# Attention with queries and keys projected transposed, stacked by DMA in two pieces, and two heads in the row halves of the array

## The reference

```python
qkv = (x @ Wqkv).reshape(b, l, 3, H, DH)          # b 8, l 512, H 16, DH 16
q, k, v = (qkv[:, :, 0], qkv[:, :, 1], qkv[:, :, 2])
q = q * cos + rotate_half(q) * sin                # rotate_half: (-second half, first half)
k = k * cos + rotate_half(k) * sin
scores = jnp.einsum('bqhd,bkhd->bhqk', q, k) * DH ** -0.5
attn = softmax(scores, axis=-1)
out = jnp.einsum('bhqk,bkhd->bqhd', attn, v).reshape(b, l, d)
x = layernorm(x + out @ Wo)
```

## Time and profile before

| | |
|---|---|
| runs of the kernel before | 1507.37 us median of 3 (1506.63 to 1508.64) |
| profiled execution | 1512.29 us, span 1510.5 us |
| TensorE busy | 1317.0 us, 87% |
| VectorE busy | 1044.7 us, 69% |
| ScalarE busy | 979.6 us, 65% |
| GpSimd busy | 518.4 us, 34% |
| granted TensorE clock, mean | 0.929 |

### The profile page before, as it was taken

The page is one execution under the profiler, slowest core; times in us unless marked ns, Lnnn a source line. Parts: engine busy times, 40 slices in busy tenths (PEclk is TensorE's granted clock), DMA queues, the critical chain, the costliest instruction groups (busy, mean ns, idle before and its releaser), DMA issues. The chain is left out here.

```text
span 1510.5 us, 30476 instructions
## 1 busy us (share of the span) xinstructions
PE 1317.0 (87%) x9849; PEld 1007.7 (67%) x9920; DVE 1044.7 (69%) x2129; ACT 979.6 (65%) x2014; POOL 518.4 (34%) x493
## 2 busy tenths in 40 slices
PE   3899999999999999689802989999999999997585
PEld 2544444444444443378702989999999999997485
DVE  3788877887888878387401557777777777775377
ACT  5588878887888888477301437666666666664265
POOL 6222212121222200064574004444444444445542
PEclk7799999999999999998955998999999999998698
DMA  8000010001000003320321006677777667762333
GB/s 335 1 1 29 2 31 1 30 1 31 2 29 2 15 1 112 123 74 18 109 104 70 0 19 233 221 221 237 238 231 239 220 219 236 235 217 63 101 102 95
DMA packets 113899, 160.46 MB, mean 106 GB/s; under 512 B 12928, under 2 KB 95872, under 8 KB 112640
## 3 DMA queue, kind: packets, MB, share of 16 engines
q1 hardware_dynamic: 107648, 142.32, 28.5%
q0 software_dynamic: 6144, 16.79, 3.5%
HBM read 121.86 MB, written 37.22 MB: 105 GB/s over the span
## 5 line engine op out<-in xcount | busy, mean ns | idle before, releaser
L470 DVE TENSOR_REDUCE att_mx<-att_psA 128x1 f32<-128x512 f32 x512 | 338.9, 682 | 62.0 <-PE att_psA L269 59.7
L387 ACT ACTIVATE att_prob<-att_psB 128x512 f32<-128x512 f32 x512 | 290.0, 602 | 81.4 <-PE att_psB L279 69.9
L1465 ACT ACTIVATE exp_psU<-exp_psU,ew_b 128x256 f32<-128x256 f32 x312 | 126.8, 444 | 154.2 <-PE exp_psU L1422 154.2
L269 PE MATMUL att_psA<-att_qk 96*128 96x512 bf16 x512 | 197.8, 388 | 8.9 <-DVE att_mx L470 5.3
L1497 DVE CAST exp_hh<-exp_psU 128x512 fp32r<-128x512 f32 x156 | 107.4, 688 | 110.2 <-ACT exp_psU L1465 110.2
L1420 PE MATMUL exp_psU<-exp_xh,exp_w1h 128*128 128x256 f32 x624 | 177.9, 285 | 2.1 <-DVE exp_w1l L1492 2.1
L1405 PE MATMUL exp_psD<-exp_w2h,exp_hh 128*128 128x256 f32 x624 | 179.6, 288 | 0.0
L1422 PE MATMUL exp_psU<-exp_xh,exp_w1l 128*128 128x256 f32 x624 | 177.5, 285 | 0.0
L1421 PE MATMUL exp_psU<-exp_xl,exp_w1h 128*128 128x256 f32 x624 | 177.5, 284 | 0.0
L279 PE MATMUL att_psB<-att_qk 128*128 128x512 bf16 x441 | 170.2, 387 | 7.8 <-issue 5.3
L1407 PE MATMUL exp_psD<-exp_w2h,exp_hl 128*128 128x256 f32 x624 | 176.5, 283 | 0.0
(11 more groups left out here) (186 smaller groups left out, 3344.1 us busy)
## 6 DMA issues: line engine op xcount, KB each, us to landing
ew_w<-ew SPq DMA_DIRECT2D x40, 1024.0 KB
exp_w<-ew SPq DMA_DIRECT2D x38, 1024.0 KB, 6.3
exp_xs<-slots_x SPq DMA_DIRECT2D x39, 256.0 KB, 6.1
slots_y<-exp_ys SPq DMA_DIRECT2D x39, 256.0 KB, 6.9
slots_x<-pre_acc SPq DMA_DIRECT2D x9, 1024.0 KB, 14.2
ew_b<-eb SPq DMA_DIRECT2D x39, 128.0 KB, 5.9
att_xt<-xT SPq DMA_DIRECT2D x8, 512.0 KB, 4.6
attn_rows<-att_ob SPq DMA_DIRECT2D x8, 512.0 KB, 3.2
```

Of the source, the lines that this page charges most:

```text
L269: pe.matmul(psA[A_BANK[n % U]][:, :], r[:, 0, qt * P:(qt + 1) * P], r[:, 1, :], start=True, stop=True).then_inc(s_amm, 1)
L387: act.activation(prob[:, n % PR, :], psB[n % 2][:, :], ACT.Exp, scale=SCALE).then_inc(s_exp, 1)
L470: dve.reduce_max(mx[:, g % 2, n % U:n % U + 1], psA[A_BANK[n % U]][:, :], AX_X).then_inc(s_max, 1)
```

## The change

Queries and keys are projected with the weights as the stationary operand, so that features lie in partitions and rows of the sequence in columns: no head has to be transposed. The weights' columns are reordered on the host, eight heads to a block, the even heads in the first 64 partitions and the odd ones in the last 64. A second product with rotated columns gives the rotated half. There are 32 blocks (four for each sequence: queries and keys of eight heads, twice), one to a period, each with twelve fp32r products of 512 columns in three steps. ScalarE copies both results out of PSUM, GpSimd multiplies with the tables, adds, and splits the sum into two fp32r pieces. SyncE writes the two pieces to memory (`bounce_block`) and reads them back with six DMAs into `qs` and `ks` (`stack_block`): three copies of 16 rows for each half, so that one fp32r product over 48 rows sums three products of pieces. Two more rows of `qs` take the two pieces of the negative maxima; these are transposed once, copied, written to memory and read back with two DMAs (`place_max`).

Both kinds of scores are now fp32r products over 48 or 50 rows, at partitions 0 to 63 for one head of a pair and 64 to 127 for the other. Row scores run A_LEAD = 29 steps ahead, and the order of the two kinds alternates, so that neighbouring matmuls are in different halves. There are two banks `psX`. The zeroing of the slots moves to the last seven periods of SyncE's queue, and the attention's outputs are loaded back after it. Ahead of the weight split VectorE sets the rows 32 to 63 of both halves of `ks` to one.

```diff
+    PAIRS = P // (2 * DH)
+    HALF = P // 2
+    KQ = 3 * DH
+    KM = KQ + 2
+    NB = 2 * D // P
+    BLOCKS = B * NB
+    SLOTS = 4
+    BOUNCE = 4
...
-    A_LEAD = U + 4
+    A_LEAD = U + 13
...
+    PROJECT_QK, EVICT_QK = (1, 2, 3), (3, 4)
+    SPLIT_MAX, TURN_MAX, COPY_MAX = 4, 6, 7
+    COPY_OUT, TURN_OUT, NORM_OUT = 5, 8, (10, 11)
+    PROJECT_V, COPY_V, SPLIT_X = 9, 11, 14
...
+    Q_PIECES, K_PIECES = (0, 1, 0), (0, 0, 1)
...
+        hl = a.sb("hl", [P, 2, 2, L], F32R)
+        qs = a.sb("qs", [P, SLOTS, PAIRS, L], F32R)
+        ks = a.sb("ks", [P, SLOTS, PAIRS, L], F32R)
...
+        mm = a.sb("mm", [P, P], F32)
+        mrow = a.sb("mrow", [2 * U, P], F32R)
...
-        psT = a.ps("psT", [P, 2, L], BF16)
-        psX = a.ps("psX", [P, 512], F32)
-        psXt = psX[:, :].bitcast(BF16)
+        psX = [a.ps(f"psX{i}", [P, L], F32) for i in range(2)]
...
+            def stack_block(i):
+                hb, kind = i // 2, i % 2
+                sp.wait_ge(s_out[kind], 16 * (hb + 1))
+                if hb == 0:
+                    sp.wait_ge(s_ones, 2)
+                if hb >= SLOTS:
+                    sp.wait_ge(s_bmm, 2 * U * (hb - SLOTS + 1))
+                if hb >= 1:
+                    sp.wait_ge(s_stk[kind], 96 * hb)
+                for half in range(2):
+                    src = qk_rows[i % BOUNCE, half * HALF:(half + 1) * HALF].rearrange("(j d) m l -> m d j l", d=DH)
+                    for m, piece in enumerate((Q_PIECES, K_PIECES)[kind]):
+                        dst = (qs, ks)[kind][half * HALF + m * DH:half * HALF + (m + 1) * DH, hb % SLOTS, :, :]
+                        sp.dma_start(dst.bitcast(F32), src[piece]).then_inc(s_stk[kind], 16)
+            def bounce_block(i):
+                sp.wait_ge(s_lo, i + 1)
+                if i >= BOUNCE:
+                    sp.wait_ge(s_stk[i % 2], 96 * ((i - BOUNCE) // 2 + 1))
+                sp.dma_start(qk_rows[i % BOUNCE], hl[:, i % 2].bitcast(F32)).then_inc(s_out[i % 2], 16)
+            def place_max(g):
+                sp.wait_ge(s_mev, g + 1)
+                sp.dma_start(max_rows[g % BOUNCE], mrow[:, :].bitcast(F32)).then_inc(s_mout, 16)
+                sp.wait_ge(s_mout, 16 * (g + 1))
+                if g >= 1:
+                    sp.wait_ge(s_min, 32 * g)
+                for half in range(2):
+                    src = max_rows[g % BOUNCE, half * U:(half + 1) * U].rearrange("(m j t) q -> m j (t q)", m=2, t=NT)
+                    dst = qs[half * HALF + KQ:half * HALF + KM, slot_of(g), 2 * (g % 2):2 * (g % 2) + 2, :]
+                    sp.dma_start(dst.bitcast(F32), src).then_inc(s_min, 16)
...
+            for p in range(-QK_LEAD, NG + 1):
+                if valid(p + QK_LEAD - 1, BLOCKS):
+                    stack_block(p + QK_LEAD - 1)
+                if p % 4 == 2 and 2 <= (p + 6) // 4 + 2 < B:
+                    b = (p + 6) // 4
+                    sp.wait_ge(s_xl, b + 1)
+                    load_x(b + 2)
+                if p % 4 == 1 and 0 <= (p - 5) // 4 < B:
+                    store_out((p - 5) // 4)
+                if valid(p + 1, NG):
+                    place_max(p + 1)
+                if valid(p + QK_LEAD, BLOCKS):
+                    bounce_block(p + QK_LEAD)
+                if p >= TAIL:
+                    sp.wait_ge(s_init, 3)
+                    for c in pieces[2 * (p - TAIL):2 * (p - TAIL) + 2]:
+                        n = min(zero.shape[1], slots.shape[1] - c)
+                        sp.dma_start(slots[:, c:c + n], zero[:, 0:n]).then_inc(s_zero, 16)
+            assert len(pieces) <= 2 * (NG - TAIL)
+            sp.wait_ge(s_zero, 16 * len(pieces))
+            for b in range(B - 1):
+                if b >= B - 3:
+                    sp.wait_ge(s_ost[b % 2], 16 * (b // 2 + 1))
+                norm.load_attention(sp, attn_out, b)
+            store_out(B - 1)
...
+                i = p + QK_LEAD
+                if not valid(i, BLOCKS):
                     return
-                b, t = tile // NT, tile % NT
-                st = terms(stack, b, t)
-                wait(pool, it, s_qrd, tile + 1, 1)
-                pool.tensor_tensor(rr[:, :], rc[:, :], rs[:, :], ALU.add).then_inc(s_rr, 1)
-                wait(pool, it, s_p1, tile + 1, 1)
-                pool.tensor_tensor(heads_of(r1), heads_of(rr), st[:, :, 0, :], ALU.subtract).then_inc(s_r1, 1)
-                wait(pool, it, s_p2, tile + 1, 1)
-                pool.tensor_tensor(st[:, 0:H, 5, :], heads_of(r1)[:, 0:H], st[:, 0:H, 4, :], ALU.subtract).then_inc(s_p3, 1)
-                wait(pool, it, s_p3, tile + 1, 1)
-                pool.tensor_tensor(st[:, H:, 2, :], heads_of(r1)[:, H:], st[:, H:, 4, :], ALU.subtract).then_inc(s_qsp, 1)
-                if t == NT - 1 and valid(tile + 1, NT * B):
-                    x_lo(b + 1, it)
+                hi, lo = hl[:, i % 2, 0, :], hl[:, i % 2, 1, :]
+                wait(pool, it, s_cev, i + 1, 1)
+                pool.tensor_tensor(rc[:, :], rc[:, :], cos[:, :], ALU.mult).then_inc(s_rc, 1)
+                wait(pool, it, s_rev, i + 1, 1)
+                pool.tensor_tensor(rs[:, :], rs[:, :], sin[:, :], ALU.mult).then_inc(s_rs, 1)
+                wait(pool, it, s_rc, i + 1, 1)
+                wait(pool, it, s_rs, i + 1, 1)
+                pool.tensor_tensor(rr[:, :], rc[:, :], rs[:, :], ALU.add)
+                v = 16 * (i // 2)
+                if it is not None:
+                    pool.wait_ge(s_out[i % 2], v + it * (16 * BODY // 2))
+                elif v > 0:
+                    pool.wait_ge(s_out[i % 2], v)
+                pool.tensor_tensor(hi, rc[:, :], rs[:, :], ALU.add).then_inc(s_hi, 1)
+                wait(pool, it, s_hi, i + 1, 1)
+                pool.tensor_tensor(lo, rr[:, :], hi.bitcast(F32), ALU.subtract).then_inc(s_lo, 1)
+                if i % NB == NB - 1 and valid(i + 1, BLOCKS):
+                    x_lo(i // NB + 1, it)
...
+                g, m = n // U, n % U
...
+                part, slot = rows_of(half, KQ), slot_of(g)
+                pe.matmul(psA[A_BANK[n % U]][:, :], qs[part, slot, pair, qt * P:(qt + 1) * P], ks[part, slot, pair, :],
+                          start=True, stop=True).then_inc(s_amm, 1)
...
+                if u == 0:
+                    wait(pe, it, s_min, 32 * (g + 1), 32)
...
+                part, slot = rows_of(half, KM), slot_of(g)
+                pe.matmul(psB[n % 2][:, :], ks[part, slot, pair, kt * P:(kt + 1) * P], qs[part, slot, pair, :],
+                          start=True, stop=True).then_inc(s_bmm, 1)
...
+            def project_qk(i, step, it):
+                b, t = i // NB, i % NB
+                x = b % 2
+                if step == 0:
+                    freed(it, s_cev, i, BLOCKS)
+                    freed(it, s_vev, i - QK_LEAD + V_LEAD, NT * B)
+                    if t == 0:
+                        pe.wait_ge(s_xl, b + 1 if it is None else b + 1 + it * 2)
+                for n in range(4 * step, 4 * step + 4):
+                    rot, c, term = n // 6, n // 3 % DC, n % 3
+                    if n == 6:
+                        freed(it, s_rev, i, BLOCKS)
+                    cols = slice((2 * t + rot) * P, (2 * t + rot + 1) * P)
+                    weights, rows = ((wh, xh), (wh, xl), (wl, xh))[term]
+                    m = pe.matmul(psX[rot][:, :], weights[:, c, cols], rows[:, x, c, :], start=(n % 6 == 0), stop=(n % 6 == 5))
+                    if n % 6 == 5:
+                        m.then_inc(s_rmm if rot else s_cmm, 1)
+            def turn_max(g, it):
+                freed(it, s_rev, g - 1 + QK_LEAD + 1, BLOCKS)
+                wait(pe, it, s_msp, g + 1, 1)
+                if it is None and g == 0:
+                    pe.wait_ge(s_init, 6)
+                pe.transpose(psX[1][:, 0:P], mm[:, :], identf[:, :]).then_inc(s_mtr, 1)
+            def turn_out(g, it):
+                freed(it, s_mev, g + 3, NG)
+                wait(pe, it, s_oev, g + 1, 1)
+                for qt in range(NT):
+                    m = pe.transpose(psX[1][:, qt * P:(qt + 1) * P], oT[:, qt * P:(qt + 1) * P], identf[:, :])
+                m.then_inc(s_otr, 1)
+            def project_v(tile, it):
+                b, t = tile // NT, tile % NT
+                freed(it, s_cev, tile - V_LEAD + QK_LEAD + 1, BLOCKS)
+                rows, cols = slice(t * P, (t + 1) * P), slice(2 * NB * P, WN)
+                for c in range(DC):
+                    pe.matmul(psX[0][:, 0:D], xh[:, b % 2, c, rows], wh[:, c, cols], start=(c == 0), stop=False)
+                    pe.matmul(psX[0][:, 0:D], xh[:, b % 2, c, rows], wl[:, c, cols], start=False, stop=False)
+                    m = pe.matmul(psX[0][:, 0:D], xl[:, b % 2, c, rows], wh[:, c, cols], start=False, stop=(c == DC - 1))
+                m.then_inc(s_vmm, 1)
...
+                    if u % 2 == 1 and valid(n + A_LEAD, NG * U):
+                        score_rows(n + A_LEAD, it)
                     if valid(n, NG * U):
                         score_cols(n, it)
```

(38 more changed lines are left out.)

315 lines of the change are left out of this document (84 added, 231 removed).

## The result

The changed kernel takes 1674.83 us (median of 4 runs, 1669.35 to 1683.46), the kernel before beside it 1508.01 us. The ratio is 1.1105, with a 95% interval of 1.1074 to 1.1137. It is slower by 167 us where 63 us less were forecast, and lies beyond the range's 1500.

A forecast was written before the change was run, and what follows sets the result against it. TensorE was taken as the bound, VectorE and ScalarE close behind. 78 + 26 x 15.5 + 4 x 12.6 + 2 x 10.5 + 6 = 558.4 against 621.0, 62.6 less, giving 1445 us; range 1398 to 1500.

The forecast's parts named there:

- the period of 15.5 us: Attention period with a projection: 15.5 us, 2.2 above TensorE's own sum of 13.3, taken 26 times.
- the fourth rival: Attention stage: the granted clock falls; a full period at the lower level costs about 11 us more; chance 0.06.
- The pair: Two fp32r score matmuls in different row halves of TensorE stream together, 0.24 us a pair, 16 pairs a period.
- The rival without overlap: Score pairs on TensorE run one after the other, 0.46 us a pair; period 16.7, time 1479; chance 0.18.
- The walk through the steps: One full period, step by step: VectorE idles about 2 us, then leads from step 4; TensorE ends step 14 at 15.5.
- four full periods without projection: Attention periods without projection: VectorE's 11.9 us and 0.7 of gaps, 12.6 each, four times.
- The start: Before the attention loop: first matmul at 19.7 us, first rows at 56, first exponential at 78 instead of 64.8.
- ScalarE's and VectorE's relief: Work removed from both engines in a period leaves VectorE 11.9 us and ScalarE 11.4.
- GpSimd and the stacking DMAs hidden: In a period, GpSimd's 6.35 us plus a quarter of 2.35, and SyncE's 1.3 MB of transfers, cost no time.
- no cost of the zeroing at the tail: Zeroing moved to the last periods: two transfers a period, 2 MB in 12.6 us, fit without loss.
- the round trip of the maxima: SyncE writes the maxima to memory and reads them back: 4.5 us, with 6.0 available.
- The third rival: Maxima return late for score columns; each us beyond the available time costs 32 us, up to 1583; chance 0.14.

The follow-up runs named there:

- e1_fill: Changed kernel plus seven thrown-away matmuls a period where TensorE stands still; 1596.65 us, ratio 1.058 to the kernel before.
- e2: Changed kernel with the output copy moved ahead of the projection copies and the max turn in the other bank; 1560.93 us, ratio 1.0344 to the kernel before.
- e3: Changed kernel with row scores 28 instead of 29 steps ahead, so both score matmuls of a step use the same row half; 1765.16 us, no ratio.
- e9_unroll: Changed kernel with two stalls removed, steps rearranged, memsets after the splits, and the loop written out; 1491.75 us, ratio 0.990 to the kernel before.
- e7_fill48: Changed kernel plus the seven thrown-away matmuls a period, over 48 rows instead of 128; 1484.22 us beside 1396.31, ratio 1.0633 to the kernel before.

## Why the prediction was wrong

Two steps failed, and each alone is more than the gain of 63 us that was forecast. One is the period of 15.5 us, which is 19.2 at full clock: 3.7 us, 26 times, 96 us. The other is the clock, 86 us. e1_fill, which kept the clock, is still 5.8% slower than the kernel before.

**The clock fell: the fourth rival, which was given 0.06.** The step that failed here is the one that reads the clock from a busy share: "New it is busy 13.3 of 15.5, 86%, in between". A full-clock period of the changed kernel is busy 16.3 of 19.2, 85%, as said, and periods without projection 13.2 of 16, 83%, at clock 1.00. The share of a period doesn't tell them apart. What the trace shows is where the idle time lies: stalls for an exponential and for the output copy leave TensorE busy 1.35 and 1.24 of 2 us, with a third for the maxima's copy right behind, and there the clock falls, 1.3 to 3.6 us ahead of the output turn in each period with a projection that loses it (the edge of the loop apart). The e1 and e2 runs show it from both sides: filling the stalls (with more work) or removing them keeps the clock. Two things stay open. The same stalls stand in the seven periods that kept the clock, so they let it fall but don't decide when. And both runs also raised the busy share of a period, to 95 and 90%; that it is the place of the idle time which counts rests on the four periods without projection, and is argued more than shown. A period with a fall costs 26.0 instead of 19.2, 7 us more, where the rival had 11 for a whole period at the lower level. From e1, the clock is worth 784.7 - 698.6 = 86 us of the 141.

The Trainium skill's page TensorE: Matmul & The Clock Gate, under "A second HAM failure mode: psum-queue depth-cycling", describes frequent short idle times between groups of matmuls that bring the clock down and up again. The trace agrees, with stalls of 0.5 to 0.9 us; the page would have spoken for this rival more than I did.

**The pair was mis-sized.** The forecast was 0.24 us for a pair, 3.84 a period. That both stream together was right. Measured is 0.34 in a row and 0.42 to 0.43 ahead of other work. With about half of the sixteen of each kind this is 6.2 us, 2.4 more, and 26 x 2.4 = 62 us are the whole forecast gain. The bf16 run shows why in part: there it is 0.23 and 0.30, with weight loads of 0.09 to 0.11 us instead of 0.18 and more. That fp32r loads at 0.12 apart would fit under the stream was taken from V matmuls over the whole array, and did not carry over. The rival without overlap, 0.46, was nearer in price and wrong in kind; e3 measures that case at 0.67 ahead of other work.

**The walk through the steps had its waits in the wrong places.** It had VectorE leading after step 4, and its own 2.2 us of interplay. It didn't walk ScalarE's queue: the output copy stands behind both projection copies, and the value product of step 6 waits for it (0.89). The output turn's wait for the copy of the maxima was in the walk, with 0.5 us of VectorE's time; it is 0.73 of TensorE's. An exponential is waited for 0.5. In sum TensorE is idle 2.9 us, not far from the 2.2, which is luck, since the waits are others. The period of 15.5 is 13.3 of work and 2.2 of waiting, the measured 19.2 is 16.3 and 2.9: of the 3.7 us between them the pair is 2.4, the waits are 0.7, and 0.6 lie in the other prices, which I can't divide further. The four full periods without projection are too long in the same way, 15.7 us at full clock for 12.6 forecast.

**The loop's edges** were in no step. TensorE stands 5.0 and 7.7 us there, against 2.46 and 2.66 before; the second:

```profile
487.52 0.79 PE L333 MATMUL att_psB<-att_qs,att_ks 50*128 50x512 f32 x1 [7.66 <-issue]
```

**The start** was walked nearly right:

```profile
2.50 6.88 DVE L537 MEMSET att_ks<- 32x8192 f32 x1 [2.50 <-issue]
...
11.14 6.88 DVE L537 MEMSET att_ks<- 32x8192 f32 x1 [1.76 <-issue]
...
22.17 0.77 PE L355 MATMUL att_psX<-att_xh,att_wh 128*128 128x512 f32 x1 [22.17 <-DVE att_xl L541]
...
51.85 2.34 POOL L280 TENSOR_TENSOR att_xl<-att_xt,att_xh 128x1024 fp32r<-128x1024 f32 x1
...
54.33 0.76 PE L355 MATMUL att_psX<-att_xh,att_wh 128*128 128x512 f32 x1 [7.88 <-POOL att_xl L280]
```

First matmul 22.2 (forecast 19.7; the second memset began 1.8 us late), GpSimd 6.4 us per block as forecast, second x split from 51.9 (from 50), first rows 58.0 (56). The rest came late: the clock was at 1.2 GHz from 49.0 to 107.0 us, so at all 29 row matmuls, and the first exponential came at 87.8, not 78. That the low clock is the reason for these 10 us is not shown by a run of its own.

**Right:** ScalarE's and VectorE's relief, GpSimd and the stacking DMAs hidden behind the start, no cost of the zeroing at the tail, and the round trip of the maxima. At the first group the way out is issued at 82.45 and the weights of the first score column are loaded at 86.73, so it took at most 4.3 us for 4.5 forecast, and no wait of TensorE in the attention is put down to it. The third rival, which got more than twice the chance of the fourth, did not happen in the changed kernel.

**Split of the 164 us.** Start 23. Clock about 86. Full-clock period 26 x 1.65 = 43 (19.17 against 17.5 without an x split), and 3 for the late x splits. The remaining 9 or so are edges of the loop and the first period; I have not separated them further.

## What to carry to other kernels

Before a change that takes work off TensorE, look not at its busy share but for places where several short stalls stand close together: there the clock can fall, and periods with as much idle time, but no such cluster, kept it here (13.2 busy of 16 us, clock 1.00). Price the period at full clock first, though: here it alone turned the gain into a loss. If a kernel has lost its clock, a few thrown-away matmuls at the stalls show within one run what the clock costs; then remove the stalls by walking every engine's queue around each single-buffered bank, the copies on ScalarE first. Splitting the array for two small matmuls pays in a run of them, less between matmuls of other shapes: a bf16 pair one after the other took 0.44 before, and the fp32r pair side by side 0.43.

## What of the hardware was not expected

Two row halves start within 10 ns of each other, yet with fp32r weights the next pair starts 0.34 us later, and with bf16 0.23. At the edge of a loop of the hardware TensorE stood 2.5 to 7.7 us, with no wait to show for it; in straight code of the same periods it didn't (e9_unroll, no stand over 0.8 us there). And one kernel took 1507 us in some sets of runs and 1396 in others, while the attention took the same time in both: with the thrown-away matmuls the last exponential starts at 698.6 us in either (e1_fill and e7_fill48), and the whole takes 1596.65 and 1484.22. The difference lies behind the attention. About half of it is this row of e1_fill's waits behind 600 us, which the trace of e7_fill48 doesn't have:

```profile
PE shr_psU L900 <- issue: 55.8, 5, 23.7
```

What makes it is not shown. The record has chip number 2 beside both times of the kernel before, so it can't be put down to the chip.
